# An LSTM step whose f and o gates are summed in PSUM: 48 small matmuls instead of 32

## The chip, the core and the metric

The kernel runs on one core of one Trainium2 chip. The metric is the device time of one execution in microseconds. Engines are named as in the profile: PE is TensorE (PEld its weight loads), DVE is VectorE, ACT is ScalarE, POOL is GpSimd, SP issues DMAs.

## The reference

A transformer block in hyperbolic space is added to the input, and an LSTM over the 512 tokens is added to that. The block is untouched by the change. The LSTM, for 4 sequences (B) of 512 steps with 256 hidden units, is

```python
a = xw_t + prev_h @ Wh                      # 4 x 1024
i, f, o = sigmoid(a[:, 0:256]), sigmoid(a[:, 256:512]), sigmoid(a[:, 512:768])
g = tanh(a[:, 768:1024])
next_c = f * prev_c + i * g
next_h = o * tanh(next_c)
return x + hs                               # hs: next_h of all steps
```

with `xw = x @ Wx + b` of the block's output. Each step needs the step before it, so 512 steps stand one behind the other.

## The kernel before

The 512 tokens are cut into 4 blocks of 128. The transformer's block j and the LSTM's steps of block j-1 are written into one program: every engine has its own instruction stream, and each stream alternates pieces of the block's work ("slots") with one LSTM step. So block 0 runs without steps (to about 470 us), blocks 1 to 3 each carry 128 steps, and the last 128 steps run alone from 1592 us on. In a block the first 68 slots are attention (L596 scores, L611 weighted sum, L853 exponentials on ACT, L342 low halves of the weights on POOL and DVE), then come projection and norms, the hidden layer (L665, L669, L679), and the gate inputs of the next 128 steps (L701 on PE, copied by L960 on ACT). Within one stream the order is fixed; between the streams there are semaphores.

An LSTM step m before the change. h (scaled, 128 partitions x 2 halves of the hidden units x 4 sequences) is kept as two fp16 numbers, high and low, side by side in `h16`; Wh likewise as two fp16 halves in `wh16`. PE waits for the low half (`l_lo`), then multiplies each 128x128 piece of Wh by the 8 columns (4 sequences x high and low): 16 products for the gates i and g into bank `pA`, 8 for f into `pF`, 8 for o into `pO` (L727). The high and the low part stand in neighbouring columns of PSUM. The gate inputs of 16 steps (a round) are put into the high columns beforehand by `put_round` (L710): after the last step of a round PE waits until `gA`, `gF`, `gO` have been read and writes the next 16 steps' inputs through an fp32 product with the identity.

DVE adds the neighbouring columns (L1265 gA, L1267 gF, L1269 gO), ACT makes tanh of each (L967 tA, L969 into `cmul`, L971 tO), DVE makes i times g (L1272 cadd) and the cell by one scan over 24 elements (L1275 cnew), ACT its tanh (L973 tC), DVE o's factor (L1278 oU), the high half of h (L1283), h in fp32 (L1284 h32), the low half (L1286), and two copies that nobody in the step waits for (L1287 cadd, L1289 hs for the output).

A scan of the triples (0, 0.5, ...) serves as a small program: each element is the previous result times one operand plus (or minus) the other, and the zero at the head of a triple restarts it.

Of the kernel before, what the change touches and what calls it, by code (L numbers as in the profile page):

```python
# [82 lines left out]
def bass_hyperbolic_block_then_lstm(nc, x, cond, w_q, b_q, w_k, b_k, w_v, b_v, w_o, b_o, w_f1, b_f1, w_f2, b_f2,  # L83
                                    w_ada, b_ada, w_x, w_h, b_l, out):
    ctx = ExitStack()
    with ctx:
# [73 lines left out]
        h16 = sb("h16", [P, KD, B, 2], F16)  # L160
        gA = sb("gA", [P, 16])
        gF = sb("gF", [P, 8])
        gO = sb("gO", [P, 8])
        h32 = sb("h32", [P, KD * B])
        tA = sb("tA", [P, 16])
        tO = sb("tO", [P, 8])
        oU = sb("oU", [P, 8])
# [346 lines left out]
        def _(pe):  # L514
# [872 lines left out]
```

## Time and profile before

| | us |
|---|---|
| median of 3 runs | 1904.62 (1903.64 to 1904.72) |
| the profiled execution | 1905.15 |
| its span | 1903.0 |
| PE busy | 1214.6 (64%) |
| DVE busy | 1174.1 (62%) |
| ACT busy | 950.6 (50%) |
| POOL busy | 404.2 (21%) |
| L727, the steps' products | 514.6 in 16384 |

The span is the stretch from the first to the last instruction that the profiler saw; the execution's own time holds some 2 us more around it. Busy shares are means over stages that are unlike each other, so the rows below go by stage. PE's busy time is modelled: a matmul's end includes the drain of the array, in which the next one can run already. An instruction on DVE or ACT likewise starts a little before the one ahead of it ends.

### The profile page before, as it was taken

To read this page: it belongs to the slowest core of one execution; us is meant where nothing else is said; L and a number is where in the kernel's file an instruction comes from. 1 tells how busy PE (TensorE), PEld (TensorE's weight loads), DVE (VectorE), ACT (ScalarE), POOL (GpSimd) and SP (SyncE) were. 2 spreads that over 40 slices of the span, in tenths; PEclk is the share of its full clock that TensorE was granted. 3 is DMA by queue.
4 is the path that set the end of the run, shared out by engine and by line. 5 is a ranking of instruction groups with operands and counts; after the bars stand their busy time and mean duration, and the time that the engine had idled before them with its cause. 6 is when DMAs were issued, how large, how long until landed. Compare 5 with 4: busy or idle time off the path is not lost.

```text
span 1903.0 us, 60748 instructions
## 1 busy us (share of the span) xinstructions
PE 1214.6 (64%) x21103; PEld 978.4 (51%) x21103; DVE 1174.1 (62%) x6657; ACT 950.6 (50%) x3287; POOL 404.2 (21%) x802
## 2 busy tenths in 40 slices
PE   4666677176777558867775588677764976444444
PEld 3544445145655445656554466555553665444443
DVE  6456634222777765657777666577776665666665
ACT  0333378234766644556666445466654554333332
POOL 4222234432221131311221312112114130000000
PEclk9667655588555557975555589655555886555555
DMA  8000000000000000000000000000000000000000
GB/s 257 0 0 0 0 1 0 1 1 1 3 0 0 2 3 2 2 25 3 0 1 3 2 2 2 25 2 0 1 2 3 2 2 13 0 0 0 0 0 13
DMA packets 14555, 17.85 MB, mean 9 GB/s; under 512 B 3348, under 2 KB 13208, under 8 KB 14360
## 3 DMA queue, kind: packets, MB, share of 16 engines
q1 hardware_dynamic: 10248, 10.50, 1.7%
q10 hardware_dynamic: 4112, 4.86, 0.9%
q8 instruction: 110, 1.80, 0.4%
q14 instruction: 85, 0.70, 0.1%
HBM read 13.25 MB, written 2.10 MB: 8 GB/s over the span
## 4 chain that ended last, share of the span: by engine, by line
PE 41%; DVE 25%; ACT 14%; issue 11%; POOL 6%; DMA 1%; POOLq 1%; ACTq 1%; DVEq 1%; SPq 0%
PE psum L727 20%; DVE cnew L1275 4%; DVE cadd L1272 4%; ACT tC L973 4%; DVE h L1283 3%; PE psum L701 3%; DVE h L1286 3%; PE psum L710 3%; DVE gO L1269 3%; PE psum L669 3%; POOL sc L226 3%; PE psum L679 2%; PE psum L559 2%; PE psum L596 2%; DVE h L1284 1%
## 5 line engine op out<-in xcount | busy, mean ns | idle before, releaser
L727 PE MATMUL psum<-h,wh 128*128 128x8 f16 x16384 | 514.6, 168 | 437.6 <-DVE h L1286 419.6
L727 PEld LDWEIGHTS psum<-h,wh 128*128 128x128 f16 x16384 | 479.7, 103 | 558.4 <-DVE h L1286 526.1
L967 ACT ACTIVATE tA<-gA 128x16 f32<-128x16 f32 x512 | 110.5, 216 | 474.5 <-DVE gA L1265 473.7
L1265 DVE TENSOR_REDUCE gA<-psum 128x16 f32<-128x32 f32 x512 | 97.4, 190 | 214.2 <-PE psum L727 213.5
L973 ACT ACTIVATE tC<-cnew 128x8 f32<-128x8 f32 x512 | 108.8, 213 | 130.9 <-DVE cnew L1275 87.3
L596 PE MATMUL psum<-qbd,kT 128*128 128x256 f16 x512 | 151.0, 400 | 24.5 <-ACT weights L853 21.5
L1272 DVE SCALAR_TENSOR_TENSOR cadd<-tA 128x8 f32<-128x8 f32 x512 | 126.8, 248 | 52.6 <-ACT tA L967 45.4
L853 ACT ACTIVATE weights<-psum 128x512 f16<-128x512 f32 x256 | 152.1, 594 | 0.0
L1283 DVE TENSOR_TENSOR h<-oU,tC 128x8 f16<-128x8 f32 x512 | 89.2, 174 | 97.1 <-ACT tC L973 96.3
L342 POOL TENSOR_TENSOR weights<-tmp,weights 128x512 f16<-128x512 f32 x64 | 74.0, 1157 | 313.2 <-ACT weights L853 313.2
L611 PEld LDWEIGHTS psum<-vs,weights 128*128 128x128 f16 x2048 | 112.3, 111 | 37.6 <-issue 17.2
L611 PE MATMUL psum<-vs,weights 128*128 (+1 forms) x2048 | 117.8, 197 | 16.3 <-DVE weights L342 16.2
L1275 DVE TENSOR_TENSOR_SCAN cnew<-cmul,cadd 128x24 f32<-128x24 f32 x512 | 107.8, 211 | 26.3
L342 POOL TENSOR_TENSOR weights<-fT,weights 128x512 f16<-128x512 f32 x64 | 74.1, 1158 | 224.7 <-ACT weights L853 224.7
L969 ACT ACTIVATE cmul<-gF 128x8 f32<-128x8 f32 x512 | 107.6, 210 | 0.0
L971 ACT ACTIVATE tO<-gO 128x8 f32<-128x8 f32 x512 | 105.5, 206 | 0.3
L1286 DVE TENSOR_TENSOR h<-h 128x8 f16<-128x8 f32 x512 | 88.7, 173 | 18.0
L1269 DVE TENSOR_REDUCE gO<-psum 128x8 f32<-128x16 f32 x512 | 88.9, 174 | 16.2
L1267 DVE TENSOR_REDUCE gF<-psum 128x8 f32<-128x16 f32 x512 | 88.7, 173 | 8.6
L226 POOL TENSOR_TENSOR sc<-sc,cst 128x2 f32<-128x2 f32 (+3 forms) x100 | 84.1, 841 | 19.5 <-POOL sc L274 10.4
L1287 DVE COPY cadd<-cnew 128x16 f32<-128x16 f32 x512 | 86.2, 168 | 0.0
L1289 DVE COPY hs<-h 128x8 f32 (+1 forms) x512 | 85.7, 167 | 0.0
(225 smaller groups left out, 2183.7 us busy)
## 6 DMA issues: line engine op xcount, KB each, us to landing
arena<-in_x_dram SPq DMA_DIRECT2D x4, 512.0 KB, 10.0
wf<-in_L_cond_w_f_dram SPq DMA_DIRECT2D x2, 1024.0 KB, 19.7
xs<-in_x_dram SPq DMA_DIRECT2D x4, 512.0 KB, 5.4
out_dram<-place SPq DMA_DIRECT2D x16, 128.0 KB, 2.1
arena<-in_L_cond_w_ada_dram ACTq DMA_DIRECT2D x1, 1536.0 KB
weights<-in_L_cond_Wh_dram ACTq DMA_DIRECT2D x1, 1024.0 KB, 14.7
gates<-in_L_cond_b_ada_dram ACTq DMA_DIRECT2D x8, 128.0 KB, 15.0
wx<-in_L_cond_Wx_dram SPq DMA_DIRECT2D x1, 1024.0 KB, 21.5
```

The costliest lines, as they stand in the source:

```text
L226: ch.link(nc.gpsimd.tensor_tensor(dst, src, cst[:, which, 0:w], ALU.pow))
L342: return engine.tensor_tensor(weights[:, buf, 1, kcs, :], w32[buf][:, half], weights[:, buf, 0, kcs, :], ALU.subtract)
L596: last = mm(bank[half][:, i * 2 * P:(i + 1) * 2 * P], tile_of(kT, b)[:, hp, kc * P:(kc + 1) * P], qbd[:, hp, :], start=True, stop=True, sk ...
L611: last = mm(sums(h), weights[:, hp % 2, wl, kc, e * P:(e + 1) * P], tile_of(vs, b)[:, kc, h, :], start=kc == 0 and wl == 0, stop=kc == NB ...
L727: last = mm(cols, wh16[:, half, kc, (g0 + g) * P:(g0 + g + 1) * P], h16[:, kc, :, :], start=False, stop=g == n - 1 and kc == KD - 1 and ha ...
L853: last = A(dst.rearrange("p a b -> p (a b)"), bank[half], ACT.Exp, scale=1.0 / (math.sqrt(HD) * QK_UP * QK_UP))
L973: A(tC[:], cnew[:, :, 2], ACT.Tanh, scale=0.5).then_inc(s["l_tC"], 1)
L1269: d.tensor_reduce(gO[:], gate_cols(pO, 2, r), axis=AX.X, op=ALU.add).then_inc(s["l_gO"], 1)
L1272: d.scalar_tensor_tensor(cadd[:, :, 2], tA[:, 0:8], 1.0, tA[:, 8:16], ALU.add, ALU.mult).then_inc(s["l_ig"], 1)
L1275: d.tensor_tensor_scan(cnew[:].rearrange("p c e -> p (c e)"), cmul[:].rearrange("p c e -> p (c e)"), cadd[:].rearrange("p c e -> p (c e)") ...
L1283: d.tensor_tensor(hi, by_k(oU), by_k(tC), ALU.mult).then_inc(s["l_hi"], 1)
L1286: d.tensor_tensor(lo, by_k(h32), hi, ALU.subtract).then_inc(s["l_lo"], 1)
```

## The change

Four things change in a step, and nothing outside it.

- h's halves move into `hl`, high and low apart, each element the third of a triple. `ot3` holds triples (0, oU, tC), and the high half's triples begin with -1.
- The low half is one scan over 24 elements of `ot3` and `hl`: 0 x state + 1, then oU x 1 - 0, then tC x oU - high. It waits for the high half (`l_hi`). h32 is gone; the copy for the output is now a product of oU and tC.
- f and o have one column of PSUM per sequence instead of two. PE multiplies them by the high half (4 columns) and by the low half (4 columns) apart, and PSUM sums all of it. gF and gO are gone from DVE: ACT reads `pF` and `pO` itself. i and g keep their 8 columns and gA.
- PE's order in a step: wait for `l_hi`, 8 products of f with the high half; wait for `l_lo`, 16 of i and g; 8 of f with the low half; 8 and 8 of o. `put_round` waits for tF and tO where it waited for gF and gO.

```diff
@@ put_round
-                for (bk, g0, n, made), read in zip(GATE_BANKS, ("l_gA", "l_gF", "l_gO")):
+                for (bk, g0, n, e), read in zip(GATE_BANKS, ("l_gA", "l_tF", "l_tO")):
...
+            def gate_products(which, r, h_of):
+
+                bk, g0, n, e = GATE_BANKS[which]
+                for g in range(n):
+                    cols = gate_cols(bk, n, e, r)[:, g * B:(g + 1) * B, :]
+                    for kc in range(KD):
+                        for half in range(2):
+                            last = mm(cols, wh16[:, half, kc, (g0 + g) * P:(g0 + g + 1) * P], h_of(kc),
+                                      start=False, stop=g == n - 1 and kc == KD - 1 and half == 1, skip_group_check=True)
+                return last
...
@@ pe_step
+                both = lambda kc: hl[:, :, kc, :, 2].rearrange("p e b -> p b e")
+                pe.wait_ge(s["l_hi"], m)
+                gate_products(1, r, lambda kc: hl[:, 0, kc, :, 2])
                 pe.wait_ge(s["l_lo"], m)
-                for bk, g0, n, made in GATE_BANKS:
-                    for g in range(n):
-                        cols = gate_cols(bk, n, r)[:, g * B:(g + 1) * B, :]
-                        for kc in range(KD):
-                            for half in range(2):
-                                last = mm(cols, wh16[:, half, kc, (g0 + g) * P:(g0 + g + 1) * P], h16[:, kc, :, :],
-                                          start=False, stop=g == n - 1 and kc == KD - 1 and half == 1, skip_group_check=True)
-                    last.then_inc(s[made], 1)
+                gate_products(0, r, both).then_inc(s["l_A"], 1)
+                gate_products(1, r, lambda kc: hl[:, 1, kc, :, 2]).then_inc(s["l_F"], 1)
+                gate_products(2, r, lambda kc: hl[:, 0, kc, :, 2])
+                gate_products(2, r, lambda kc: hl[:, 1, kc, :, 2]).then_inc(s["l_O"], 1)
...
@@ act_step
-                act.wait_ge(s["l_gF"], m)
-                A(cmul[:, :, 1], gF[:], ACT.Tanh, scale=down).then_inc(s["l_tF"], 1)
-                act.wait_ge(s["l_gO"], m)
-                A(tO[:], gO[:], ACT.Tanh, scale=down).then_inc(s["l_tO"], 1)
+                act.wait_ge(s["l_F"], m)
+                A(cmul[:, :, 1], gate_cols(pF, 2, 1, r)[:, :, 0], ACT.Tanh, scale=down).then_inc(s["l_tF"], 1)
+                act.wait_ge(s["l_O"], m)
+                A(tO[:], gate_cols(pO, 2, 1, r)[:, :, 0], ACT.Tanh, scale=down).then_inc(s["l_tO"], 1)
...
@@ dve_step
-                d.tensor_reduce(gF[:], gate_cols(pF, 2, r), axis=AX.X, op=ALU.add).then_inc(s["l_gF"], 1)
...
-                d.tensor_reduce(gO[:], gate_cols(pO, 2, r), axis=AX.X, op=ALU.add).then_inc(s["l_gO"], 1)
...
-                d.tensor_tensor(hi, by_k(oU), by_k(tC), ALU.mult).then_inc(s["l_hi"], 1)
-                d.tensor_tensor(h32[:], oU[:], tC[:], ALU.mult).then_inc(s["l_h32"], 1)
-                v.wait_ge(s["l_h32"], m)
-                d.tensor_tensor(lo, by_k(h32), hi, ALU.subtract).then_inc(s["l_lo"], 1)
+                by_k = lambda t: t.rearrange("p (k b) -> p k b", b=B)
+                d.tensor_tensor(hcol, by_k(oU), by_k(tC), ALU.mult).then_inc(s["l_hi"], 1)
+                v.wait_ge(s["l_hi"], m + 1)
+                d.tensor_tensor_scan(lo3, ot3[:].rearrange("p c e -> p (c e)"), hi3, 0.0, ALU.mult, ALU.subtract).then_inc(s["l_lo"], 1)
```

What this does to the streams, first on PE in the hidden layer of a block, two steps with the squared norm (usq) and one first-layer product (wf, uT) between them. Before:

```order
L727 MATMUL psum<-h,wh 128x8 [waits s_l_lo]
L727 MATMUL psum<-h,wh 128x8 x31
L658 MATMUL psum<-ones,usq 128x1 [waits s_t_us]
L658 MATMUL psum<-ones,usq 128x1
L669 MATMUL psum<-wf,uT 128x512
L721 REGISTER_ALU
L727 MATMUL psum<-h,wh 128x8 [waits s_l_lo]
L727 MATMUL psum<-h,wh 128x8 x31
```

The same place on PE after the change (the file's lines have moved by a few):

```order
L724 MATMUL psum<-hl,wh 128x4 [waits s_l_hi]
L724 MATMUL psum<-hl,wh 128x4 x7
L724 MATMUL psum<-hl,wh 128x8 [waits s_l_lo]
L724 MATMUL psum<-hl,wh 128x8 x15
L724 MATMUL psum<-hl,wh 128x4 x24
L656 MATMUL psum<-ones,usq 128x1 [waits s_t_us]
L656 MATMUL psum<-ones,usq 128x1
L667 MATMUL psum<-wf,uT 128x512
L731 REGISTER_ALU
L724 MATMUL psum<-hl,wh 128x4 [waits s_l_hi]
L724 MATMUL psum<-hl,wh 128x4 x7
L724 MATMUL psum<-hl,wh 128x8 [waits s_l_lo]
```

A step's products stand in one piece as before; 8 of 4 columns now stand ahead of those of 8 columns and 24 behind them, where 16 of 8 columns stood behind.

Second, DVE's part of one step in the last 128. Before:

```order
L1265 TENSOR_REDUCE gA<-psum 128x16 [waits s_l_A]
L1267 TENSOR_REDUCE gF<-psum 128x8 [waits s_l_F]
L1269 TENSOR_REDUCE gO<-psum 128x8 [waits s_l_O]
L1272 SCALAR_TENSOR_TENSOR cadd<-tA 128x8 [waits s_l_tA]
L1275 SCALAR_TENSOR_TENSOR cnew<-cmul,cadd 128x24 [waits s_l_tF,s_l_ig]
L1278 TENSOR_SCALAR oU<-tO 128x8 [waits s_l_tO]
L1283 TENSOR_TENSOR h<-oU,tC 128x8 [waits s_l_oU,s_l_tC]
L1284 TENSOR_TENSOR h<-oU,tC 128x8
L1286 TENSOR_TENSOR h<-h 128x8 [waits s_l_h32]
L1287 COPY cadd<-cnew 128x8x2
L1289 ISA
L1289 COPY hs<-h 128x8
```

DVE's part of the same step after the change:

```order
L1277 TENSOR_REDUCE gA<-psum 128x16 [waits s_l_A]
L1280 SCALAR_TENSOR_TENSOR cadd<-tA 128x8 [waits s_l_tA]
L1283 SCALAR_TENSOR_TENSOR cnew<-cmul,cadd 128x24 [waits s_l_tF,s_l_ig]
L1286 TENSOR_SCALAR ot<-tO 128x8 [waits s_l_tO]
L1290 TENSOR_TENSOR hl<-ot 128x8 [waits s_l_oU,s_l_tC]
L1291 REGISTER_ALU
L1292 SCALAR_TENSOR_TENSOR hl<-ot,hl 128x24 [waits s_l_hi]
L1293 COPY cadd<-cnew 128x8x2
L1295 ISA
L1295 TENSOR_TENSOR hs<-ot 128x8
```

Three instructions are gone, two ahead of cadd and h32 behind h; the scan (L1292) stands where the low half stood.

## Rows read from the trace of the kernel before

**Rows 1.** Busy time by stage: us; engines' busy us (x instructions); PE clock; DMA.

```profile
1101.30:1152.70 51.40, 49.04 (x735) 35.50 (x736) 35.52 (x230) 28.65 (x117) 11.13 (x32) 0.93 0.01 2
1592.40:1860.00 267.60, 127.02 (x3626) 115.95 (x3626) 168.05 (x1233) 93.00 (x448) 0.00 (x0) 0.50 0.00 0
```

**Rows 2.** Timeline, a plain step: start us, us, engine, line, operation, [idle before].

```profile
1752.39 0.17 DVE L1283 TENSOR_TENSOR h<-oU,tC 128x8 f16<-128x8 f32 x1 [0.17 <-ACT tC L973]
1752.67 0.17 DVE L1286 TENSOR_TENSOR h<-h 128x8 f16<-128x8 f32 x1
1752.89 0.93 PEld L727 LDWEIGHTS psum<-h,wh 128*128 128x128 f16 x32 [1.43 <-DVE h L1286]
1753.53 0.19 DVE L1265 TENSOR_REDUCE gA<-psum 128x16 f32<-128x32 f32 x1 [0.53 <-PE psum L727]
1753.75 0.22 ACT L967 ACTIVATE tA<-gA 128x16 f32<-128x16 f32 x1 [1.39 <-DVE gA L1265]
1753.95 0.21 ACT L969 ACTIVATE cmul<-gF 128x8 f32<-128x8 f32 x1
1753.95 0.17 DVE L1269 TENSOR_REDUCE gO<-psum 128x8 f32<-128x16 f32 x1
1754.04 0.16 DVE L1272 SCALAR_TENSOR_TENSOR cadd<-tA 128x8 f32<-128x8 f32 x1
1754.16 0.21 ACT L971 ACTIVATE tO<-gO 128x8 f32<-128x8 f32 x1
1754.26 0.21 DVE L1275 TENSOR_TENSOR_SCAN cnew<-cmul,cadd 128x24 f32<-128x24 f32 x1
1754.50 0.21 ACT L973 ACTIVATE tC<-cnew 128x8 f32<-128x8 f32 x1
1754.75 0.17 DVE L1283 TENSOR_TENSOR h<-oU,tC 128x8 f16<-128x8 f32 x1 [0.17 <-ACT tC L973]
```

**Rows 3.** Timeline of PE at the end of a round, last 128 steps.

```profile
1779.81 2.07 PE L710 MATMUL psum<-arena,ident 128*128 x6
1781.67 1.04 PE L727 MATMUL psum<-h,wh 128*128 128x8 f16 x32
```

**Rows 4.** Timeline, attention: beside POOL's L342; a round's second step.

```profile
969.48 1.16 POOL L342 TENSOR_TENSOR weights<-tmp,weights 128x512 f16<-128x512 f32 x1 [4.08 <-ACT weights L853]
969.94 0.72 DVE L1272 SCALAR_TENSOR_TENSOR cadd<-tA 128x8 f32<-128x8 f32 x1
971.68 0.93 PEld L727 LDWEIGHTS psum<-h,wh 128*128 128x128 f16 x32 [0.86 <-DVE h L1286]
977.77 1.04 PE L727 MATMUL psum<-h,wh 128*128 128x8 f16 x32
```

**Rows 5.** L1272 in one attention: count: shortest/median/longest ns, first, last start.

```profile
L1272 DVE SCALAR_TENSOR_TENSOR cadd<-tA x64: 157/170/1118, 846.7 to 1021.1; 128x8 f32<-128x8 f32 x64
```

**Rows 6.** Timeline of PE in the hidden layer, pieces of three steps.

```profile
1121.07 1.10 PE L669 MATMUL psum<-wf,uT 128*128 128x512 f32 x2
1122.12 0.96 PE L727 MATMUL psum<-h,wh 128*128 128x8 f16 x32
1122.93 1.96 PE L669 MATMUL psum<-wf,uT 128*128 128x512 f32 x4
1124.73 0.94 PE L727 MATMUL psum<-h,wh 128*128 128x8 f16 x32
...
1130.72 0.60 PE L679 MATMUL psum<-wf,fT 128*128 128x256 f32 x2
1131.74 0.95 PE L727 MATMUL psum<-h,wh 128*128 128x8 f16 x32 [0.42 <-DVE h L1286]
```

**Rows 7.** L727 by line, hidden layer, gate inputs: busy us, mean ns | idle us.

```profile
L727 PE MATMUL psum<-h,wh 128*128 128x8 f16 x609 | 18.4, 167 | 2.9 <-DVE h L1286 2.9
...
L727 PE MATMUL psum<-h,wh 128*128 128x8 f16 x512 | 15.4, 167 | 5.7 <-DVE h L1286 3.5 <-ACT arena L960 1.9
```

**Rows 8.** Timeline of ACT in the gate inputs.

```profile
1184.42 1.62 ACT L960 ACTIVATE arena<-psum,blc,unit 128x128 f32 x4 [1.45 <-PE psum L701]
```

More of the change, by code:

```diff
@@ L158, in bass_hyperbolic_block_then_lstm @@
         big1 = sb("big1", [P, 8])
-        h16 = sb("h16", [P, KD, B, 2], F16)
+        hl = sb("hl", [P, 2, KD, B, 3], F16)
         gA = sb("gA", [P, 16])
-        gF = sb("gF", [P, 8])
-        gO = sb("gO", [P, 8])
-        h32 = sb("h32", [P, KD * B])
         tA = sb("tA", [P, 16])
         tO = sb("tO", [P, 8])
-        oU = sb("oU", [P, 8])
+        ot3 = sb("ot3", [P, KD * B, 3])
         cmul = sb("cmul", [P, 8, 3])
@@ L283, in bass_hyperbolic_block_then_lstm, with gate_cols @@
         UNIT = (0.5,) * 2 + (1.0,) * 2 + (0.5,) * 4
-        GATE_BANKS = ((pA, 0, 4, "l_A"), (pF, 4, 2, "l_F"), (pO, 6, 2, "l_O"))
-        def gate_cols(bk, n, r):
-            return bk[:, r * n * B * 2:(r + 1) * n * B * 2].rearrange("p (c e) -> p c e", e=2)
+        GATE_BANKS = ((pA, 0, 4, 2), (pF, 4, 2, 1), (pO, 6, 2, 1))
+        def gate_cols(bk, n, e, r):
+            return bk[:, r * n * B * e:(r + 1) * n * B * e].rearrange("p (c e) -> p c e", e=e)
         WLOADS = 8
@@ L705, in pe_gates, with put_gates @@
                     pe_gates_T(n + 1, b + 1)
-            def put_gates(bk, g0, n, first):
+            def put_gates(bk, g0, n, e, first):
                 part = (xw[:, first:first + ROUND, g0:g0 + n, :] if isinstance(first, int) else xw[:, bass.ds(first, ROUND), g0:g0 + n, :])
-                mm(bk[:, 0:ROUND * n * B * 2].rearrange("p (t c e) -> p t c e", t=ROUND, e=2)[:, :, :, 0], ident[:], part.rearrange("p t g b -> p t (g b)"),
+                mm(bk[:, 0:ROUND * n * B * e].rearrange("p (t c e) -> p t c e", t=ROUND, e=e)[:, :, :, 0], ident[:], part.rearrange("p t g b -> p t (g b)"),
@@ L773, in _ @@
             pe.wait_ge(s["l_x0"], 1)
-            for bk, g0, n, made in GATE_BANKS:
-                put_gates(bk, g0, n, 0)
+            for bk, g0, n, e in GATE_BANKS:
+                put_gates(bk, g0, n, e, 0)
             with pe.Fori(1, NB) as j:
@@ L1264, in dve_step @@
                 v.wait_ge(s["l_A"], m)
-                d.tensor_reduce(gA[:], gate_cols(pA, 4, r), axis=AX.X, op=ALU.add).then_inc(s["l_gA"], 1)
-                v.wait_ge(s["l_F"], m)
-                d.tensor_reduce(gF[:], gate_cols(pF, 2, r), axis=AX.X, op=ALU.add).then_inc(s["l_gF"], 1)
-                v.wait_ge(s["l_O"], m)
-                d.tensor_reduce(gO[:], gate_cols(pO, 2, r), axis=AX.X, op=ALU.add).then_inc(s["l_gO"], 1)
+                d.tensor_reduce(gA[:], gate_cols(pA, 4, 2, r), axis=AX.X, op=ALU.add).then_inc(s["l_gA"], 1)
                 v.wait_ge(s["l_tA"], m)
@@ L1277, in dve_step @@
                 v.wait_ge(s["l_tO"], m)
-                d.tensor_scalar(oU[:], tO[:], 1.0, 0.5 * H_UP, ALU.add, ALU.mult).then_inc(s["l_oU"], 1)
+                d.tensor_scalar(oU, tO[:], 1.0, 0.5 * H_UP, ALU.add, ALU.mult).then_inc(s["l_oU"], 1)
                 v.wait_ge(s["l_tC"], m)
                 v.wait_ge(s["l_oU"], m)
-                hi, lo = (h16[:, :, :, half] for half in range(2))
-                by_k = lambda t: t[:].rearrange("p (k b) -> p k b", b=B)
-                d.tensor_tensor(hi, by_k(oU), by_k(tC), ALU.mult).then_inc(s["l_hi"], 1)
-                d.tensor_tensor(h32[:], oU[:], tC[:], ALU.mult).then_inc(s["l_h32"], 1)
-                v.wait_ge(s["l_h32"], m)
-                d.tensor_tensor(lo, by_k(h32), hi, ALU.subtract).then_inc(s["l_lo"], 1)
+                by_k = lambda t: t.rearrange("p (k b) -> p k b", b=B)
+                d.tensor_tensor(hcol, by_k(oU), by_k(tC), ALU.mult).then_inc(s["l_hi"], 1)
+                v.wait_ge(s["l_hi"], m + 1)
+                d.tensor_tensor_scan(lo3, ot3[:].rearrange("p c e -> p (c e)"), hi3, 0.0, ALU.mult, ALU.subtract).then_inc(s["l_lo"], 1)
                 d.tensor_copy(cadd[:, :, 0:2], cnew[:, :, 2:3].to_broadcast([P, KD * B, 2])).then_inc(s["l_cc"], 1)
-                d.tensor_copy(hs[:, :, :, i:i + 1] if isinstance(i, int) else hs[:, :, :, bass.ds(i, 1)],
-                              h32[:].rearrange("p (k b o) -> p k b o", b=B, o=1)).then_inc(s["l_hs"], 1)
+                d.tensor_tensor(hs[:, :, :, i:i + 1] if isinstance(i, int) else hs[:, :, :, bass.ds(i, 1)],
+                                by_k(oU).unsqueeze(3), by_k(tC).unsqueeze(3), ALU.mult).then_inc(s["l_hs"], 1)
             def dve_out(j):
```

17 lines of the change are left out of this document (11 added, 6 removed).

## Prediction

> **What bounds the kernel now.** I read the stretches first. In the last quarter (128 LSTM steps and nothing else) TensorE is busy 127.0 of 267.6 us at a granted clock of 0.50 (1.2 GHz); in the hidden layer of a block it is busy 49.0 of 51.4 us at 0.93 [rows 1]. So there are two regimes: a chain of dependent small instructions, and a TensorE that is full.
>
> The chain is seen in the timeline of one plain step [rows 2], from h at 1752.39 to h at 1754.75, 2.36 us. Its links, by their starts: h (fp16 high half) 1752.39, the low half 1752.67, first weight load 1752.89, reduction gA 1753.53, tanh tA 1753.75, cadd 1754.04, scan 1754.26, tC 1754.50, h 1754.75. The reduction gO starts when the 32nd product is done and gA when the 16th is, 0.42 us apart: a product pair (load and matmul) costs 0.42/16 = 0.0267 us at this clock. The last loads of the step end 0.93 us after its first [rows 2], so from there to 1754.75 TensorE has nothing to do.
>
> The other regime is the hidden layer [rows 6]: the recurrent product at 1124.73 follows L669 with no idle time before it. The row that groups this stretch gives 609 products, 19 steps, with 2.9 us of idle time before them in all [rows 7], where one plain step of the last quarter leaves TensorE 1.4 us (2.36 less 0.93). There the pace is 0.81/32 = 0.0253 us a pair (1122.12 to 1122.93).
>
> **The change in a plain step.** Three parts.
>
> First, the start of the i,g product. Before, h32 and then the low half: the weights load 0.50 us after h (1752.39 to 1752.89). Now one scan waits for h itself. h takes 0.17, waking 0.04 (as tC's end to h, 1754.71 to 1754.75), the scan of 24 elements 0.21 (that of cnew in the same rows), waking TensorE 0.05: 0.47. Gain 0.03. The eight products of f with h's high half may start at 0.17 + 0.05 = 0.22 and end at 0.22 + 8 x 0.0267 = 0.44, just ahead of 0.47: hidden here. The scan's price is bounded by 0.17 (the old low half) and 0.21; I take 0.21, the same operation.
>
> Second, gF and gO leave VectorE. cadd started at 1754.04, 0.09 after gO, the spacing of back-to-back VectorE instructions; tA had ended at 1753.97, so it could have started near 1754.01. Gain 0.03. The scan waits for cadd (ends 1754.20) more than for tF (ends 1754.16), so nothing more comes of tF.
>
> Third, tF and tO read PSUM. l_F now comes after 24 products counted from the i,g start, as before, and l_O after 40 instead of 32: 0.63 + 24 x 0.0267 = 1.27 after the start, 0.64 after gA. tO started 0.63 after gA (1754.16): the same within 0.01, and tC, 0.97 after gA, still waits for the scan. An activation of 8 elements costs 0.21 from SBUF; from PSUM I know it only between 0.17 and 0.21, and either end is hidden. The cover is thin: about 0.08 us before tO would hold tC.
>
> Together -0.06 us for a plain step.
>
> **What it adds where TensorE is full.** 48 pairs instead of 32, and two places where they hurt: 8 pairs ahead of the i,g product (f, high half) and 8 more behind it (16 become 24: f with the low half 8, o 16). A step whose TensorE is full pays all 16: 0.41 us warm, 0.43 at half clock; one that has a slack s pays 0.42 - s, and one with 0.45 or more pays nothing. No row has a pair with 4 columns: it may cost half of one with 8, or the same. I take the same, since 8 columns show a pace set by the load, not by the columns (0.0253 and 0.0267 at clocks that differ twofold). The Trainium skill, "TensorE: Matmul & The Clock Gate", section "Back-to-back issue gap", lists one floor of about 25 ns for anything from 1 to 64 columns; an estimate by that page is 16 x 0.025 = 0.40 us a full step, and the sum below would be 0.5 us lower.
>
> **The sum, stage by stage.**
>
> Last quarter: 120 plain steps x -0.06 = -7.2. At 7 of them a round of 16 steps ends and TensorE first writes the next gate inputs, L710 from 1779.81 to the next product at 1781.67 [rows 3]: TensorE is late there, so 0.43 - 0.03 = +0.40 each, +2.8. Sum -4.4.
>
> Attention with steps, 64 to 68 a block [rows 5]. Every second step has cadd held up, 0.72 instead of 0.16 us, until GpSimd's L342 ends (969.48 + 1.16 = 970.64, cadd ends 970.66) [rows 4]. GpSimd is released by ScalarE's exponentials, which follow tC, so a gain between tC and cadd is swallowed: 0. TensorE has 0.86 us of idle time ahead of the next product there (971.68), so the 16 pairs are hidden too. Counted in the block from 845 us: 22 plain steps, -1.3; four that wait for VectorE's normalising, -0.1; four ends of rounds, where VectorE lets the inputs be written late and only the 8 leading pairs count, 4 x 0.18 = +0.7; three steps right behind them, with no idle time (977.77) [rows 4], 3 x 0.40 = +1.2. Sum +0.5, in three blocks +1.5.
>
> Projection and norms, 24 steps a block: 10 plain -0.6, 7 held by VectorE -0.2, one end of a round +0.4, two products behind the f32 projection +1.0: +0.6, in three blocks +1.8.
>
> Hidden layer [rows 6, 7], 19 steps: seven are like 1124.73, late behind f32 products: 7 x 0.41 = 2.9. Five are like 1122.12, ready 1.05 us after two L669 that take 0.95 of it (half of 1.80, the time of four at 1122.93 to 1124.73), so a slack of about 0.1: 5 x 0.30 = 1.5. Five are like 1131.74, with 0.35 to 0.65 idle, to which about 0.15 of drain is to be added since a busy time of 0.95 stands against a pace of 0.81: 5 x -0.03 = -0.15. Two end in a long wait for GpSimd: 0. Sum 4.2.
>
> Gate inputs of the next block [rows 7, 8], 16 steps and the loop's turn: the first six by the same rule +1.15 (0.21, 0.32, 0.28, -0.03, 0.40, -0.03). In the others ScalarE's copies L960 wait for L701 (idle 1.45) and the step's tA stands behind them on ScalarE. The pairs ahead of the i,g product come after L701 and are hidden; those behind it delay the next L701. I followed each step: +2.0. Sum 3.15, with the hidden layer 7.35, in three blocks +22.
>
> Total: -4.4 + 1.5 + 1.8 + 22 = +20.9. The profiled execution took 1905.15 us (span 1903.0 and 2.15 around it), 0.5 above the median of the runs: 1926.0 against it, **1925.5** as a median. Bounds: the last term is 6 if only the leading pairs of the late steps count, some 32 if every step of the two stretches pays in full; the plain gain is 0 to 0.09 a step over some 215 steps, +13 to -6 against the sum. So 1905 to 1940 for this mechanism.
>
> **Rivals.**
>
> *The extra pairs are free (faster).* If a pair were paid by its columns, nothing is added: 16 x 8 + 32 x 4 = 256 = 32 x 8. Then every boundary and full step keeps the plain gain: -7.6, -4.4, -2.4, and -0.03 x 35 x 3 = -3.2, total -17.6, 1887. It decides wherever the row before a product shows no idle time. For it: equal columns. Against it: the pace of 0.0253 to 0.0267. 0.05. A half-way case, the f32 work waiting for ScalarE and VectorE often enough to hide most of the pairs, ends near 1899: 0.06.
>
> *The clock rises.* A step has half as many products again; if the granted clock went from 0.50 to full in the last quarter and the attention, a pair would cost 0.0253, the product would be ready 0.03 earlier, and the inputs' 1.86 us at 1779.81 would halve, so that the rounds' ends no longer hold anything: about 0.045 x 180 + 0.9 x 19 = 25 less, 1900. Against it: TensorE was busy 48% there at 0.50 [rows 1] and the columns stay the same. 0.05. The Trainium skill, "TensorE: Matmul & The Clock Gate", Part 1, says that activity releases the clock; by that rule it would come out so, and the row, half a clock at half a time busy, does not yet bear it out.
>
> *The clock falls.* The hidden layer holds 0.93 [rows 1] with f32 products in about two thirds of its time; with more small pairs among them it may drop to half. Four L669 would then take 3.6 instead of 1.8 us, some 1.2 us more on average in 19 steps of three blocks, +68: 1993 at most, 1950 if it drops for a part of the time. 0.05.
>
> *Nothing to see.* Chain gains and full steps cancel, if the slack in the full steps is larger than I read: within 0.2% of 1904.6. 0.05.
>
> **Chances.** My forecast has 0.74. Runs of this kernel tell differences of about 0.2% (3.8 us). Faster: 0.05 and 0.04 of the half-way case, 0.02 of the clock: 0.11. Same: 0.05, what these two leave (0.02 and 0.03), and 0.02 for the forecast's own low edge: 0.12. Slower: 0.72 and 0.05 of the falling clock: 0.77. The range leaves out the free pairs and the falling clock: 1903 to 1940.
>
> **What would show it.** In the last quarter: plain steps of 2.29 to 2.30 instead of 2.36, ends of rounds near 3.3 instead of 2.89. In the attention: pairs of steps still 2.3 and 2.89, with cadd still held to the end of L342. In the hidden layer: 0.41 us from the last product of i,g to the next f32 matmul more than before, no idle time before products, and steps of 2.7 to 3.0 where they were 2.3 to 2.6. If the products with 4 columns run at half the pace of the others, or tO ends after the scan in a plain step, the forecast falls.

## The result, and the profile after

The changed kernel takes 1962.22 us (median of 4 runs, 1957.72 to 1969.54) where the kernel before takes 1904.13 beside it: a ratio of 1.0309, 95% interval 1.0277 to 1.0341. The sign of the forecast was right, its size was not: 58 us more instead of 21, outside the range of 1903 to 1940. Ratios here and below are of fast executions; one execution of experiment 5's kernel, 4709 us at a granted clock of 0.18, is in the slow state.

The profiled execution took 1957.72 us, 52.6 above that of before. Its page, busy time of the engines and the queue that brings instructions (packets, MB, share):

```profile
PE 1450.3 (74%) x29295; PEld 1227.5 (63%) x29295; DVE 1031.7 (53%) x5123; ACT 887.0 (45%) x3287; POOL 403.2 (21%) x802
...
q8 instruction: 210, 3.44, 0.7%
```

The same row on the page of before:

```profile
q8 instruction: 110, 1.80, 0.4%
```

That is 110 packets before and 210 after. This is the row that the forecast did not read.

By stage, counted between the starts of the 512 instructions that make h (L1290, before L1283), in us against the kernel before, blocks 1 / 2 / 3:

| stage | forecast per block | after |
|---|---|---|
| attention, 67 steps | +0.5 | +7.3 / +7.2 / +7.7 |
| projection and norms, 25 | +0.6 | +2.0 / +1.3 / +2.0 |
| hidden layer and gate inputs, 36 | +7.35 | +13.0 / +8.3 / +14.6 |
| last 127 steps, once | -4.4 | -8.6 |

That makes +54.7. The first h comes 0.3 earlier, and 1.5 is gained behind the last one; the spans differ by 52.9 (1955.9 against 1903.0). Against the forecast's +20.9 the attention is 20.7 above, hidden layer and gate inputs 13.8 above, the projection 3.5 above, and the last quarter 4.2 below.

**The last quarter.** It still runs at half clock, busier than in [rows 1] (us; busy us of the engines; granted clock):

```profile
1684.00:1895.00 211.00, 143.18 (x4381) 134.62 (x4379) 111.36 (x727) 61.52 (x364) 0.00 (x0) 0.50 0.00 0
```

A plain step there, to be laid beside [rows 2]:

```profile
1752.53 0.17 DVE L1290 TENSOR_TENSOR hl<-ot 128x8 f16<-128x8 f32 x1
1752.74 0.21 DVE L1292 TENSOR_TENSOR_SCAN hl<-ot,hl 128x24 f16<-128x24 f32 x1
1752.76 1.38 PEld L724 LDWEIGHTS psum<-hl,wh 128*128 128x128 f16 x48 [0.88 <-DVE hl L1290]
...
1753.63 0.19 DVE L1277 TENSOR_REDUCE gA<-psum 128x16 f32<-128x32 f32 x1 [0.54 <-PE psum L724]
1753.86 0.21 ACT L975 ACTIVATE tA<-gA 128x16 f32<-128x16 f32 x1 [1.36 <-DVE gA L1277]
1753.98 0.16 ACT L977 ACTIVATE cmul<-psum 128x8 f32<-128x8 f32 x1
1754.11 0.17 DVE L1280 SCALAR_TENSOR_TENSOR cadd<-tA 128x8 f32<-128x8 f32 x1 [0.28 <-ACT tA L975]
1754.27 0.18 ACT L979 ACTIVATE tO<-psum 128x8 f32<-128x8 f32 x1
1754.31 0.21 DVE L1283 TENSOR_TENSOR_SCAN cnew<-cmul,cadd 128x24 f32<-128x24 f32 x1
1754.48 0.17 DVE L1286 TENSOR_SCALAR ot<-tO 128x8 f32<-128x8 f32 x1
1754.55 0.21 ACT L981 ACTIVATE ot<-cnew 128x8 f32<-128x8 f32 x1
1754.80 0.17 DVE L1290 TENSOR_TENSOR hl<-ot 128x8 f16<-128x8 f32 x1
```

From h to h it is 2.27 us, where it was 2.36. The scan now starts 0.03 after cadd ends (1754.28); in [rows 2] it starts 0.06 after cadd ends, but 0.10 after tF ends. The end of a round is still set by the next gate inputs, as in [rows 3]:

```profile
1800.35 2.05 PE L708 MATMUL psum<-arena,ident 128*128 x6
1802.19 1.47 PE L724 MATMUL psum<-hl,wh 128*128 128x4 f16 x48
```

Such a step takes 3.18 us (2.89 before).

**The attention.** Every second step is still the 2.89 us that [rows 4, 5] explain. But in each block there are two steps of 7.5 to 8.3 us where the kernel before has 4.16. TensorE's timeline at one of them, block 2:

```profile
917.61 0.61 PE L594 MATMUL psum<-qbd,kT 128*128 128x256 f16 x2
921.40 0.48 PE L724 MATMUL psum<-hl,wh 128*128 128x4 f16 x12 [3.18 <-issue]
924.37 1.12 PE L724 MATMUL psum<-hl,wh 128*128 128x8 f16 x36 [2.49 <-issue]
```

"issue" is time in which the engine waited for nothing that the profile shows: no semaphore, no data. It waited 3.18 us ahead of a step's products and 2.49 more in the middle of them. This is where the loop of `along_attention` jumps back, twice a block. In the changed kernel the instruction queue brings a 16 KB packet every 3 to 7 us all through the attention. Before the change it is silent from the first jump back to the loop's end (893.7 to 992.0 us in block 2). The DMA of 900 to 985 us, in block 2's attention, before and after:

```profile
DMA packets 0, 0.00 MB, mean 0 GB/s; under 512 B 0, under 2 KB 0, under 8 KB 0
```

```profile
q8 instruction: 18, 0.29, 1.4%
```

**The hidden layer** (its 24 steps in each block; us, PE busy, granted clock), which [rows 1] gives at 0.93:

```profile
736.60:815.80 79.20, 76.88 (x1314) 0.84 0.01 3
1133.70:1208.30 74.60, 72.31 (x1314) 0.91 0.01 3
1526.80:1604.00 77.20, 74.90 (x1314) 0.89 0.01 3
```

The work is the same in all three, the clock is not, and the lower the clock, the longer the time. In block 2 the row that groups the recurrent products there, as in [rows 7], has no idle time left before them:

```profile
L724 PE MATMUL psum<-hl,wh 128*128 128x4 f16 (+1 forms) x1152 | 33.6, 167 | 0.0
```

### The profile page after: what moved, and what is told of

Read it like the earlier page. It is cut to its first block, busy times and chain, and to the rows that moved or that the text cites. A ratio compares the mean times of both kernels' runs of the same rounds, so it can differ in the third digit from the quotient of the medians.

```text
span 1955.9 us, 75622 instructions
## 1 busy us (share of the span) xinstructions
PE 1450.3 (74%) x29295; PEld 1227.5 (63%) x29295; DVE 1031.7 (53%) x5123; ACT 887.0 (45%) x3287; POOL 403.2 (21%) x802
## 4 chain that ended last, share of the span: by engine, by line
PE 42%; DVE 22%; ACT 16%; issue 12%; POOL 6%; DMA 1%; ACTq 1%; POOLq 1%; DVEq 0%; SPq 0%
PE psum L724 18%; DVE cadd L1280 5%; DVE cnew L1283 4%; ACT tA L975 4%; PE psum L699 3%; PE psum L667 3%; ACT ot L981 3%; PE psum L708 3%; DVE hl L1290 3%; PE psum L677 3%; DVE gA L1277 3%; POOL sc L224 2%; PE psum L594 2%; PE psum L557 2%; ACT weights L861 2%
## 5 line engine op out<-in xcount | busy, mean ns | idle before, releaser
L724 PEld LDWEIGHTS psum<-hl,wh 128*128 128x128 f16 x24576 | 718.7, 103 | 390.0 <-DVE hl L1290 303.9
L724 PE MATMUL psum<-hl,wh 128*128 128x4 f16 (+1 forms) x24576 | 747.0, 169 | 281.1 <-DVE hl L1290 229.9
L981 ACT ACTIVATE ot<-cnew 128x8 f32<-128x8 f32 x512 | 109.4, 214 | 125.0 <-DVE cnew L1283 87.9
L1290 DVE TENSOR_TENSOR hl<-ot 128x8 f16<-128x8 f32 x512 | 90.7, 177 | 90.3 <-ACT ot L981 64.3
L1283 DVE TENSOR_TENSOR_SCAN cnew<-cmul,cadd 128x24 f32<-128x24 f32 x512 | 115.3, 225 | 18.6 <-DVE cadd L1280 1.0
L1292 DVE TENSOR_TENSOR_SCAN hl<-ot,hl 128x24 f16<-128x24 f32 x512 | 107.9, 211 | 18.4 <-DVE hl L1290 0.9
L979 ACT ACTIVATE tO<-psum 128x8 f32<-128x8 f32 x512 | 90.9, 178 | 47.9
L1295 DVE TENSOR_TENSOR hs<-ot 128x8 f32 (+1 forms) x512 | 85.5, 167 | 0.0
L977 ACT ACTIVATE cmul<-psum 128x8 f32<-128x8 f32 x512 | 84.5, 165 | 0.4
L557 PE MATMUL psum<-place,uT 128*128 128x256 f32 x204 | 84.6, 598 | 0.0
L1286 DVE TENSOR_SCALAR ot<-tO 128x8 f32<-128x8 f32 x512 | 83.9, 164 | 0.1
## 6 DMA issues: line engine op xcount, KB each, us to landing
weights<-in_L_cond_Wh_dram ACTq DMA_DIRECT2D x1, 1024.0 KB, 14.2
```

The lines of the kernel that those rows point to most:

```text
L981: A(tC, cnew[:, :, 2], ACT.Tanh, scale=0.5).then_inc(s["l_tC"], 1)
L1283: d.tensor_tensor_scan(cnew[:].rearrange("p c e -> p (c e)"), cmul[:].rearrange("p c e -> p (c e)"), cadd[:].rearrange("p c e -> p (c e)") ...
L1290: d.tensor_tensor(hcol, by_k(oU), by_k(tC), ALU.mult).then_inc(s["l_hi"], 1)
```

## Experiments

My theory after the result: about 22 us of the 37 that were missing are TensorE waiting for its own instructions after the jump back, since the loop body has outgrown what TensorE keeps; most of the rest is the lower clock in the hidden layer. The rivals: the sixteen pairs' own time in the attention, and something in the split itself.

**1. The jump taken away.** TensorE's side of the attention stage is written out:

```
+            if step and unrolled:
+                for b in range(B - 1):
+                    base = eng.snap(carried(j, b * PAIR_SLOTS))
+                    for q in range(LEAD, PAIR_SLOTS + LEAD):
+                        step(base + q, b * PAIR_SLOTS + q, q % ROUND)
...
-                along_attention(pe, j, step, pe_attention)
+                along_attention(pe, j, step, pe_attention, unrolled=True)
```

> The changed kernel, with TensorE's side of the attention stage in blocks 1 to 3 written out (three passes of 16 steps in a row) in place of a loop that jumps back twice per block; the other engines keep their loops and the work is the same. Theory A (the missing time is TensorE waiting for its own instructions after the jump back, 7.7 to 8.3 us for a step that else takes 4.2, six times): the six long steps fall to about 4.2 us, attention costs +0 to +1 us per block against the kernel before in place of +7.1, the time falls by 6 x 3.6 = 21.6 us to about 1936 to 1941 us. Rival B (the sixteen pairs' own execution in the busy attention stage): nothing moves, 1958 to 1963 us. Rival C (straight code is fetched no faster than code behind a jump): the stall is spread over all steps of the stage, attention stays at +7 us per block, 1958 to 1963 us.

Measured: 1935.76 us, ratio 1.0163 (1.0146 to 1.0180), 26 us less than with the loop. The long steps are 4.16 us again and the attention costs -2.2 us per block instead of +7.4, where theory A expected 0 to +1. In the profiled executions the attention gives back 28.8 us in three blocks, the span only 22.6: hidden layers and gate inputs cost 5.9 more than with the loop (+12.3 / +14.7 / +14.7), and the clock was at its low level for 135 us of them instead of 123. The rows of the products in block 2's attention (busy us, mean ns | idle us before, by releaser), first with the loop, then written out:

```profile
L724 PE MATMUL psum<-hl,wh 128*128 128x4 f16 (+1 forms) x3216 | 98.8, 169 | 28.6 <-DVE hl L1290 17.0 <-issue 11.3
...
L609 PE MATMUL psum<-vs,weights 128*128 (+1 forms) x512 | 27.9, 197 | 1.2 <-DVE weights L340 1.2
```

```profile
L734 PE MATMUL psum<-hl,wh 128*128 128x4 f16 (+1 forms) x3216 | 98.6, 169 | 24.7 <-DVE hl L1300 24.5
...
L619 PE MATMUL psum<-vs,weights 128*128 128x33 f16 x512 | 20.8, 193 | 3.6 <-DVE weights L350 3.6
```

The 11.3 us of "issue" are gone. Rivals B and C fall: the pairs are as many, and straight code, which is fetched all the time too (194 packets), does not wait. But the version has a second gain: the 512 attention products take 20.8 instead of 27.9 us, since their addresses are no longer worked out in registers between them (a pass of the loop has 104 or 105 FUSED_REGOPS instructions on TensorE, 16 steps written out 5 or 6). It shows in the three steps a block that follow the end of a round, 2.27 us written out and 2.80 in the loop. So of 9.6 us a block about 7.7 belong to the jumps and 1.6 to this.

**2. f alone, o alone.** One of the two gates is put back (8 columns, a reduce on VectorE): 40 matmuls a step, 811 in the loop's body instead of 939 (683 before).

```
-        GATE_BANKS = ((pA, 0, 4, 2), (pF, 4, 2, 1), (pO, 6, 2, 1))
+        GATE_BANKS = ((pA, 0, 4, 2), (pF, 4, 2, 1), (pO, 6, 2, 2))
...
+                v.wait_ge(s["l_O"], m)
+                d.tensor_reduce(gO[:], gate_cols(pO, 2, 2, r), axis=AX.X, op=ALU.add).then_inc(s["l_gO"], 1)
```

(f alone; o alone is its mirror, and there nothing starts before the low half of h.)

> The changed kernel with the o gate put back: o's products again take both halves of h in 8 columns (8 matmuls fewer, 40 a step), VectorE adds the two halves (one reduce more), ScalarE reads o from SBUF. f stays split and its high half leads. TensorE's attention loop body is then 811 matmuls in place of 939 (683 before). Theory A: no long step at the jump back (all six at 4.2 to 4.4 us), attention +0 to +1 us per block; hidden layer and gate inputs about half of what the change cost in block 2 (+7.8), so +3 to +5 per block; the step in the tail loses some of the 0.09 us; together 1908 to 1920 us. Rival B (cost by pairs): attention +3.5 us per block, half of +7.1, 1928 to 1935 us. If the long steps are still there in full, the jump costs whatever the length of the body, and A as a matter of size is wrong: 1935 us or more.

> The changed kernel with the f gate put back: f's products again take both halves of h in 8 columns behind those of i and g, VectorE adds them (one reduce more), ScalarE reads f from SBUF; nothing starts before the low half of h. o stays split. 40 matmuls a step, loop body of 811 matmuls as in the kernel with f alone. Theory A: no long step, attention +0 to +1 us per block; the hidden layer and gate inputs about +3 to +5 per block, since o is last in the step and has slack in a plain step; together 1905 to 1920 us. Rival B: attention +3.5 us per block, 1925 to 1935 us.

Measured: 1947.41 us, ratio 1.0228 (1.0211 to 1.0245), and 1945.56, ratio 1.0212 (1.0181 to 1.0243). Both missed what the theory expected: the long steps are there with 811 too, so the bound lies lower than I had set it. Hidden layer and gate inputs cost +7.3 / +4.5 / +9.4 and +6.8 / +6.9 / +6.7, where +3 to +5 was expected. The products' rows in block 2's attention, f alone and o alone:

```profile
L725 PE MATMUL psum<-hl,wh 128*128 128x8 f16 (+1 forms) x2680 | 84.5, 170 | 35.1 <-DVE hl L1292 28.2 <-issue 6.9
```

```profile
L725 PE MATMUL psum<-hl,wh 128*128 128x8 f16 (+1 forms) x2680 | 82.6, 170 | 38.4 <-DVE hl L1293 31.8 <-issue 6.6
```

TensorE waits a second time here too, 1.3 to 1.9 us ahead of the next attention products.

In the last quarter a plain step takes 2.300 us with f alone and 2.326 with o alone; both together 2.267.

**3. The scan alone.** 32 matmuls, both reduces, and only the low half of h from the scan (the edit as read against the kernel before).

```
-                d.tensor_tensor(h32[:], oU[:], tC[:], ALU.mult).then_inc(s["l_h32"], 1)
-                v.wait_ge(s["l_h32"], m)
-                d.tensor_tensor(lo, by_k(h32), hi, ALU.subtract).then_inc(s["l_lo"], 1)
+                d.tensor_tensor_scan(lo3, ot3[:].rearrange("p c e -> p (c e)"), hi3, 0.0, ALU.mult, ALU.subtract).then_inc(s["l_lo"], 1)
```

> Of the change only the way in which the low half of h is made (one scan behind the high half, in place of a product and a subtraction) and the layout of h that goes with it; f and o are not split: 32 matmuls a step, both reduces are back. Theory A and my price of the scan (0.03 us a step earlier products): a tail step of 2.32 to 2.35 us against 2.36, no long steps, about 0.03 x 512 = 15 us less at most, 1889 to 1904 us. Rival (the scan saves nothing, or reading h with a stride slows the products): 1904 to 1915 us.

Measured: 1902.59 us, ratio 0.9984 (0.9975 to 0.9994). A plain step takes 2.326 instead of 2.355, 0.029 less: the 0.03 of the forecast. The last quarter gains 3.0 us, an attention 0.9, and no step is long (110 packets).

**4. Length alone, and the jump alone.** The kernel before, its step untouched, with its loop body lengthened by matmuls of 4 columns into a place that is overwritten at once (16 of them: 811 in the body; 11: 771); and the kernel before written out as in 1.

```
                 pe.wait_ge(s[f"t_e{half}"], HP * k + hp + 1)
+                if half == 1 and longer and not isinstance(b, int):
+                    for i in range(16):
+                        mm(bank[half][:, 0:4], tile_of(kT, b)[:, hp, 0:P], qbd[:, hp, 0:4], start=True, stop=True, skip_group_check=True)
```

> The kernel before (32 matmuls a step, gates joined), with 128 matmuls of 4 columns more in the body of TensorE's attention loop of blocks 1 to 3: sixteen ahead of the scores of every second step, into columns that the scores then overwrite. The body so has 811 matmuls, as in the kernels with f or o alone; before it has 683, and the loop over the last steps of the changed kernel, which shows no long steps, has 771. They stand in steps in which TensorE has about 0.9 us to spare, at 0.4 us each. Theory A (it is the length of the loop body, whatever is in it): the steps behind the two jumps back grow by 3 to 4 us each, and nothing else by much: attention +6 to +9 us per block, 1923 to 1932 us. Rival B (the long steps come from what the change does to the step, f and o apart or the lead of f's high half): no long steps, 1904 to 1911 us.

> As the lengthened kernel before, with 88 in place of 128 extra matmuls in the body of TensorE's attention loop: 771 matmuls, the number in the loop over the last steps of the changed kernel, which refetches nothing. 811 gave 3.3 us of TensorE waiting for instructions at the first jump, 683 none. If 771 still fits: no instruction fetches within the loop, no such wait, 1904 to 1910 us. If not, the bound lies between 683 and 771 for this loop, whose body has some 110 instructions more that are no matmuls: fetches all through, the same 3.3 us wait at each jump, 1914 to 1920 us.

> The kernel before with TensorE's attention stage of blocks 1 to 3 written out, as in the unrolled changed kernel. Theory A: the jump back costs nothing while the body is short, so nothing moves: 1903 to 1907 us. Rival (writing the stage out is worth something whatever the body's length, so that the unrolled changed kernel had two gains): 1890 to 1900 us.

Measured: with 811, 1919.58 us, ratio 1.0069 (1.0053 to 1.0084); with 771, 1906.14, ratio 1.0002 (0.9992 to 1.0011); written out, 1903.26, ratio 0.9999 (0.9977 to 1.0022; one of its ten executions took 1924.92). With 811, TensorE at the first jump, then the products' row in block 2's attention:

```profile
521.19 0.59 PE L599 MATMUL psum<-qbd,kT 128*128 128x256 f16 x2
525.05 1.01 PE L730 MATMUL psum<-h,wh 128*128 128x8 f16 x32 [3.27 <-issue]
```

```profile
L730 PE MATMUL psum<-h,wh 128*128 128x8 f16 x2080 | 66.6, 169 | 40.1 <-DVE h L1289 32.7 <-issue 7.0
```

With 771, the same row, and the queue on its page:

```profile
L730 PE MATMUL psum<-h,wh 128*128 128x8 f16 x2160 | 68.8, 168 | 39.6 <-DVE h L1289 39.3
```

```profile
q8 instruction: 112, 1.84, 0.4%
```

So length alone makes the wait, and it comes whole between 771 and 811 matmuls: none, or 3.2 to 3.5 us at each of the six jumps. What it costs is another matter. Here the long step is 5.5 us, only 1.3 over its 4.16, since TensorE had slack there; I had expected 3 to 4, and the time came out below the range. The attention costs +4.5 a block, part of it for the added matmuls themselves: with 771 and no wait it costs +0.9. In the changed kernel TensorE waits a second time, inside the products, and the step grows by 3.6. Written out, the kernel before has the same attention within 0.1 us a block, so neither the jump nor the shorter attention products count where TensorE has time.

**5. The lead of f's high half taken away.** The written-out kernel with f's eight leading products behind those of i and g.

```
-                pe.wait_ge(s["l_hi"], m)
-                gate_products(1, r, lambda kc: hl[:, 0, kc, :, 2])
                 pe.wait_ge(s["l_lo"], m)
                 gate_products(0, r, both).then_inc(s["l_A"], 1)
+                gate_products(1, r, lambda kc: hl[:, 0, kc, :, 2])
```

> The unrolled changed kernel, with the eight products of f with the high half of h put behind those of i and g: nothing starts before the low half of h. Reading the tail of the changed kernel: the step waits for the chain i and g, their tanh, the product of the two, the scan; tanh of f is done 0.14 us before that product, so f may end 0.2 us later. Theory: the lead is worth nothing, a plain tail step stays at 2.26 to 2.28 us, 1930 to 1941 us. Rival (the lead carries the gain of the tail): a plain step of 2.30 to 2.47 us, 1945 us or more.

Measured: 1961.89 us, ratio 1.0293 (1.0274 to 1.0312), a plain step of 2.440 us: my theory on the lead fell. I had followed f and forgotten o, which stands behind it. The timeline of a plain step there, ScalarE and VectorE from tO on:

```profile
1756.66 0.18 ACT L988 ACTIVATE tO<-psum 128x8 f32<-128x8 f32 x1 [0.24 <-PE psum L734]
1756.76 0.21 ACT L990 ACTIVATE ot<-cnew 128x8 f32<-128x8 f32 x1
1756.87 0.17 DVE L1295 TENSOR_SCALAR ot<-tO 128x8 f32<-128x8 f32 x1
1757.15 0.17 DVE L1299 TENSOR_TENSOR hl<-ot 128x8 f16<-128x8 f32 x1
```

tO now waits for TensorE (idle 0.24), oU comes 0.11 behind tC's start instead of 0.07 ahead of it, and h waits for oU, which ends at 1757.04, while tC has ended at 1756.97. The lead is worth 0.17 us a step, because it takes eight pairs out of the way of o; without it the split would lose in the last quarter as well (+12.1 instead of -8.6).

**6. Each form where it pays.** The 48-matmul step in the first 64 steps of each block and in the last 128, joined gates (32 matmuls, the scan kept) in the other 64 of each block, TensorE's attention written out.

```
+        SPLIT, JOINED = (((pA, 0, 4, 2), (pF, 4, 2, e), (pO, 6, 2, e)) for e in (1, 2))
+        APART = 4
...
+                form = lambda x: SPLIT if (APART if not isinstance(x, int) else x < APART * ROUND) else JOINED
```

> A kernel of both parts: the changed kernel's step (48 matmuls) in the first 64 steps of each block, in which attention lies, and in the last 128 steps; in the other 64 steps of each block, with the projection, the hidden layer and the gate inputs, f and o are joined again (32 matmuls, both reduces) and only the scan stays. TensorE's attention stage is written out. Theory (the loss is the jump back, and the extra pairs where TensorE is the bound): attention -2 us per block and tail -8.6 as in the unrolled kernel, the rest within +-1 us per block as with the scan alone: 1905 - 6 - 8.6 = about 1890 us, 1886 to 1895. Rival (the low clock of the hidden layer comes from the attention stage's extra pairs and not from its own): the hidden layer and gate inputs keep +6 to +12 us per block, 1908 us or more.

Measured: 1892.83 us (median of 5), ratio 0.9931 (0.9917 to 0.9945): faster than the kernel before and the changed one, in the range expected. Attention -2.0 per block, last quarter -8.6, projection -0.3 / -1.0 / -0.5, hidden layer +0.8 / +3.2 / +1.1, gate inputs within 0.6. So the rival falls: of its +6 to +12 in the hidden layer and gate inputs +0.5 to +3.7 is there.

**7. The clock of the hidden layer.** The mixed kernel with wide matmuls done twice there, as much TensorE time as the sixteen pairs:

```
+                    more_wide = (2 - half if kc == 0 else 0) if not isinstance(n, int) else 0
+                    for again in range(more_wide):
+                        mm(bank[half][:, :], uT[:, 0, kc, :], wf1[:, kc, half * 512:(half + 1) * 512], start=True, stop=True)
```

(and the first product into bank[4] once more).

> The mixed kernel (32 matmuls a step in the hidden layer), with four matmuls more for each of the hidden layer's tiles, each a first product of a group done again: three of 512 columns and one of 256 (685 and 428 ns each in this stage), 2.5 us of TensorE per tile, 9.9 us per block, about what the sixteen pairs add there (24 steps of 0.41 us). TensorE is busy nearly all of that stage, so they should cost about 8 to 11 us per block: 1917 to 1926 us. What is told apart is the clock there: with 48 matmuls a step and the stage written out it was low for 12.4, 14.6 and 22.3 us of the three hidden layers, in the mixed kernel for 11.2, 13.6 and 8.5. Theory P (many small matmuls bring the clock down): low for 7 to 12 us with wide ones, as in the mixed kernel. Rival L (the low stretches come at their own pace, and a longer stage takes in more of them): low for 12 to 22 us.

Measured: 1912.71 us, ratio 1.0039 (1.0027 to 1.0052), below what I expected: the hidden layer costs 4.5 to 9.7 us a block more than in the mixed kernel, not 8 to 11. The hidden layer's stretches (us; busy us of PE, PEld, DVE, ACT, POOL; granted clock) with 48 matmuls and written out, with 32 (mixed), and with the wide ones:

```profile
727.70:802.60 74.90, 72.58 (x1314) 57.20 (x1313) 39.96 (x219) 32.33 (x144) 14.40 (x42) 0.91 0.01 3
1114.70:1191.70 77.00, 74.72 (x1314) 58.39 (x1313) 40.02 (x218) 32.30 (x144) 14.38 (x42) 0.89 0.01 3
1504.10:1584.80 80.70, 78.39 (x1314) 60.88 (x1313) 40.24 (x218) 32.66 (x144) 14.32 (x42) 0.84 0.01 3
```

```profile
724.50:794.40 69.90, 65.30 (x928) 47.28 (x928) 45.95 (x266) 35.41 (x144) 14.57 (x42) 0.89 0.01 2
1098.40:1170.60 72.20, 66.14 (x928) 47.44 (x928) 45.91 (x266) 35.42 (x144) 14.57 (x42) 0.89 0.01 2
1474.80:1545.10 70.30, 64.14 (x928) 46.44 (x928) 45.87 (x266) 35.41 (x144) 14.70 (x42) 0.91 0.01 2
```

```profile
724.80:801.50 76.70, 73.38 (x961) 51.81 (x960) 45.90 (x266) 35.80 (x144) 14.61 (x42) 0.96 0.01 2
1107.70:1184.40 76.70, 73.38 (x961) 51.82 (x960) 45.89 (x267) 35.80 (x144) 14.55 (x42) 0.96 0.01 2
1486.90:1566.90 80.00, 76.68 (x960) 53.84 (x960) 45.87 (x267) 35.80 (x144) 14.54 (x42) 0.93 0.01 2
```

With wide work the clock was higher, not lower, in stretches as long as those with 48 matmuls: it was at its low level for 6.1, 5.5 and 12.0 us of them, and rival L falls. That small matmuls pull it down is not shown. By the same count the kernel with 48 was low for 14.2, 16.4 and 26.3 us and the mixed one for 14.8, 16.4 and 12.1, so only block 3 tells them apart. And the kernel with the scan alone, 32 matmuls a step, has a block 3 as low as any of these but one:

```profile
1475.80:1548.00 72.20, 67.30 (x929) 48.01 (x928) 45.94 (x266) 35.59 (x144) 14.42 (x42) 0.86 0.01 2
```

Its blocks 1 and 2 have 0.94 and 0.93, like the kernel before; the 48-matmul kernels ran the same work at anything from 0.84 to 0.93 (the highest in experiment 5). What chooses among these stays open. What it costs can be read: the 1314 matmuls of the changed kernel and the one written out take 74.6 and 74.9 us at 0.91, 77.1 and 77.2 at 0.89, 79.2 and 80.7 at 0.84, that is about 0.7 us for each 0.01 between the ends.

## Why the prediction was right or wrong

**The step that failed: the attention, +0.5 a block.** The terms that it had were good. Every second step stayed at 2.89 with the pairs hidden; three of the four ends of rounds cost 0.16 (forecast 0.18), the first nothing; the steps behind them 0.42 to 0.45 (0.40); the plain ones -0.09 (-0.06). Without the jumps block 2's attention would be at about -0.3. The term that was missing is TensorE's supply of instructions: the steps on either side of a jump grew from 4.16 to 7.7 and from 2.35 to 2.55 in block 2, 3.7 to 3.8 us a jump there, six times in all. Experiments 1 and 4 show it. No sentence of the forecast counted the loop's body or read the instruction queue, and none of its rivals had this mechanism; the count (683 matmuls before, 939 after, each with a weight load) and the 110 packets of before were there to be read.

The Trainium skill, "Runtime: NRT & Kernel Launch", section "Instruction fetch mechanics", says that TensorE's store holds 2048 instructions, that it is refilled in blocks of 256, and that a taken branch to a target outside the current window of two pages makes the engine wait for the fetch. The runs agree on the wait, with 3.15 to 3.7 us at the 24 jumps of the four kernels that have it. They do not agree on the window: a pass of 1689 instructions jumps back without a wait, one of 1769 waits (774 and 814 matmuls as the trace counts them, as many weight loads, and 141 others; the program's 771 and 811 leave out that each of three fp32 products stands there as two). So what is kept here is at least 1689 instructions, and a pass of 1769 is already too long.

**The clock, a rival with 0.05.** "It may drop to half" came true for a part of the time, 0.84 to 0.91 instead of 0.93 on average; that the small pairs are the reason is not shown (experiment 7). It took effect in blocks 1 and 3: in the first through the hidden layer (0.84, its 24 steps +10.0), in the third through the hidden layer (0.89, +7.9) and the gate inputs (+6.6, with 27 us of their 51 at half clock; +3.0 and +2.8 in the other blocks, with 20). Near the clock of before the term holds: block 2, whose hidden layer ran at 0.91, cost +8.3 for both stages (7.35 forecast). So the pair's price was right: with 4 columns 0.0256 us in block 2's hidden layer and 0.0267 in the last quarter, the same as with 8 (only the eight leading pairs of a plain step take 0.030). The search for steps without idle time was right too.

**Projection and norms, +0.6: too small.** It cost 1.3 to 2.0. Part of it is again the clock. Block 1's projection, before:

```profile
653.90:727.50 73.60, 35.11 (x837) 30.61 (x837) 46.99 (x310) 32.87 (x137) 23.19 (x65) 0.55 0.01 2
```

and after the change:

```profile
661.00:736.60 75.60, 48.05 (x1236) 43.34 (x1236) 40.05 (x236) 30.46 (x137) 23.11 (x65) 0.50 0.01 3
```

With 32 matmuls the clock was up for 3 to 7 of these 74 us in most blocks, with 40 or 48 in none; with the scan alone it was up in blocks 1 and 2, which took 72.8 us each, and not in block 3, which took 74.1. That is 1.4 us. Taken off the +2.0 of blocks 1 and 3, where the clock was up for 6.8 us before the change, it leaves the +0.6 of the forecast; no run shows the two parts separately.

**The last quarter, -4.4: right sign, half the size.** The scan's 0.03 was right (experiment 3). The other 0.03 was put down to cadd, with "nothing more comes of tF". That step was wrong: before, the scan waited for tF, which needs 0.10 us from its end to the scan's start (1754.16 to 1754.26 in [rows 2]), where cadd needs 0.03. With o alone cadd is 0.05 earlier than with the scan alone, and the scan is not:

```profile
1751.40 0.21 ACT L976 ACTIVATE cmul<-gF 128x8 f32<-128x8 f32 x1
1751.45 0.17 DVE L1281 SCALAR_TENSOR_TENSOR cadd<-tA 128x8 f32<-128x8 f32 x1
1751.71 0.21 DVE L1284 TENSOR_TENSOR_SCAN cnew<-cmul,cadd 128x24 f32<-128x24 f32 x1
```

The scan starts 0.10 after tF here too, and the step takes 2.326 us as with the scan alone; with f alone tF is earlier and the step falls to 2.300, cadd now the last; with both it is 2.267. The 0.10 is not the way from ScalarE: tA's end to cadd after the change, and tC's end to h, are 0.03 to 0.04. The scan waits for two semaphores, and the wait for tF is an instruction of its own in VectorE's queue ahead of it:

```profile
L1274 DVEq EVENT_SEMAPHORE  x512: 21/21/21, 469.5 to 1894.8; - x171
```

On average in the plain steps of before it starts 0.04 after tF's end, takes 0.02, and the scan starts 0.04 after it. In experiment 5 the same holds for a result of VectorE itself: h waits for oU by such an instruction and starts some 0.10 after oU's end (1757.04 to 1757.15 above). Rounds' ends cost +0.29 instead of +0.40. The thin cover of tO was named, and experiment 5 shows what lies under it.

**The rest.** The pairs were not free, the clock did not rise with them, and no stage but the attention without its jumps came out at nothing. The median lies 4.5 us above the profiled execution, and one run 12 above; which stage these lose in has no trace.

## What to carry to other kernels

Before adding instructions to a loop, count its body on each engine and look whether the instruction queue is silent inside it: a body that just fits costs nothing at the jump, and 40 matmuls more cost 3.2 to 3.5 us of waiting at each. Where an instruction waits for two results, look which of them is awaited by an instruction of its own in the queue: here that one needed 0.10 us from its end to the start, from either engine, and the other 0.03 to 0.04. And a form that trades TensorE's time for a shorter chain is worth having in the stages where TensorE waits, and only there.

## What the runs showed of the hardware

- A loop pass of 771 matmuls on TensorE (1689 instructions in the trace) was kept over a jump back: no packet between the first jump and the loop's end. Passes of 811 (1769) and 939 were fetched anew each time, with a wait of 3.15 to 3.7 us at the jump. A second wait follows in the changed kernel (2.2 to 2.7 us in the products) and with f or o alone (1.3 to 1.9 us ahead of the attention products), not in the lengthened kernel before.
- Sixteen attention products of block 2 take 0.86 to 1.14 us in the loop and 0.59 to 0.67 us with fixed addresses.
- A result that VectorE awaits by an instruction of its own ahead of the one that needs it took 0.10 us from its end to that one's start (tF, and oU in experiment 5); one awaited directly 0.03 to 0.04 us (cadd, tA, tC).
- ScalarE's tanh of 8 elements takes 0.16 (f) and 0.18 us (o) from PSUM, 0.21 from SBUF [rows 2].
- The same 1314 matmuls of the hidden layer got a granted clock of 0.84, 0.89 or 0.91 in the blocks of one execution; with wide f32 matmuls added it was 0.93 to 0.96, and with 32 matmuls a step 0.86 to 0.94.
